# Layer norm 2 folded into centred expert and gate weights, in an attention and mixture-of-experts layer on one core

## Chip, cores and metric

The program runs on one core of a Trainium2 chip. Its time is the device time of one execution in microseconds (us). Engines are named as the profile names them: PE (TensorE matmul) and PEld (its weight load), DVE (VectorE), ACT (ScalarE), POOL (GpSimd), SP (SyncE, which issues most DMAs).

## What is computed

Four sequences of 1024 rows of 128 numbers (float32) pass one pre-norm layer:

```
x = x + attention(layernorm(x))      # 8 heads of 16; silu on q, k, v, u; silu(scores) for softmax; gated by silu(U)
x = x + ffn(layernorm(x))
# ffn: logits = xt @ w_gate.T ; top 2 of 8 ; softmax over the two -> gates
#      y = sum_e gates[:, e] * ((xt @ w_in[e].T) @ w_out[e].T)
# layernorm(x) = (x - mean) / sqrt(var + 1e-5), no scale or offset
```

An expert has no nonlinearity, so its two matrices can be multiplied once into one 128x128 matrix, and the FFN of a row is linear in the row apart from the choice and the gates.

## The kernel before

The 4096 rows are cut into nine units of query rows: two of 512 for each of batches 0 to 2, then 512, 256 and 256 for batch 3 (UNITS, numbered 0 to 8). Attention of a unit goes in groups: a group is one stretch of up to 512 columns of scores for four heads. There are 73 groups (units 0 to 8 have 5, 13, 5, 13, 5, 13, 5, 6 and 8). For each group PE makes four score tiles (scores, L623), DVE adds the relative bias where keys are near (add_bias, L914), ACT applies silu (weigh, L782 and L784), and PE multiplies by V (times_v, L639) into o_acc. DVE then gates a finished unit (gate_outputs, L929).

All other work is cut into jobs, and a table written out by hand (BEFORE, BESIDE, AFTER) says beside which group each job is issued. Every engine walks the same table in order, each with its own part of a job, and waits only on semaphores. In a group PE issues the scores of the next group's first two heads, times_v of the group before, the jobs, and then the other two heads. ACT runs the jobs of group i while it is in group i+1, between its two pairs of heads. On DVE the jobs that drain a PSUM bank come in group i; jobs without a bank (stats, norm, best, gates, split) come in group i+1, after the bias of the first pair of group i+2. POOL runs its parts strictly in the order of the table. Two PSUM banks (jobp) serve the jobs in turn, so a job of PE waits until the job two before it is drained.

The jobs that matter here:

- WT e, M e: transposes the output matrix of expert e and multiplies the two matrices into mm_e[:, e] (PE, copied by ACT at L850 and L854).
- T1, Q, K, V, U, MASK, split, REL: layer norm 1 transposed, projections, key mask, splitting of q and k, and the bias difference for far blocks (REL, POOL L583).
- SEL u: transposes the gated attention back and adds it to xs (PE L709, DVE L995). xs then holds the sum that layer norm 2 works on.
- stats2 u: mean and variance (DVE L953, L956), then on POOL rstd = (var + eps)^-0.5 and shift = -mean * rstd (function scale, L507 to L513).
- norm2 u: ACT writes xn2 = rstd * xs + shift (L797). For the last unit DVE only subtracts the mean (L969) and rstd is applied later (L1071, L1089).
- T2 u: PE transposes xn2 (L677), ACT copies to xn2T (L808).
- LOG u: logits (PE, DVE copy L1001). best u: top two, in two parts, with gap = top1 - top2 (DVE, L1063 to L1080). tanh u: ACT, L844. gates u: DVE, L1086 to L1092, which first waits for tanh.
- FF b t part: one tile of 128 rows times four experts (PE L648). DVE scales it by the gates into ymix (L1026), POOL adds the eight experts and xs (add_experts, L565 and L567). The last two tiles are done by DVE instead (MIX, mix_last, L1040), with no ymix.

Of the kernel before, what the change touches and what calls it, by code (L numbers as in the profile page):

```python
# [144 lines left out]
BESIDE = [
    [("T1", 0, 1), ("U", 0, 0), ("stats1", 1, 0), ("WT", 0)],
    [("M", 0), ("stats1", 1, 1), ("WT", 1)],
    [("Q", 0, 1), ("K", 0, 1), ("norm1", 1, 0), ("M", 1), ("V", 0, 1), ("T1", 1, 0), ("norm1", 1, 1)],
    [("K", 1, 0), ("Q", 1, 0)],
    [("WT", 2), ("split", 1, 0), ("REL",), ("U", 0, 1)],  # L150
    [("T1", 1, 1), ("WT", 3)],
    [("M", 2), ("SEL", 0), ("stats2", 0)],
    [("Q", 1, 1), ("MASK", 0, 1)],
    [("U", 1, 0), ("norm2", 0)],
    [("K", 1, 1), ("T2", 0), ("split", 1, 1)],
    [("WT", 4), ("M", 3)],
    [("LOG", 0), ("best", 0, 0), ("V", 1, 0), ("M", 4)],
    [("WT", 5), ("tanh", 0)],
    [("M", 5), ("WT", 6)],
    [("MASK", 1, 0), ("best", 0, 1)],  # L160
    [("gates", 0)],
    [("WT", 7)],
    [("stats1", 2, 0), ("MASK", 1, 1), ("M", 6)],
    [("M", 7), ("V", 1, 1), ("FF", 0, 0, 0), ("norm1", 2, 0), ("FF", 0, 0, 1), ("SEL", 1)],
    [("FF", 0, 1, 0), ("T1", 2, 0)],
    [("FF", 0, 1, 1), ("stats2", 1), ("U", 1, 1)],
    [("K", 2, 0), ("Q", 2, 0)],
    [("FF", 0, 2, 0), ("split", 2, 0), ("norm2", 1), ("stats1", 2, 1), ("FF", 0, 2, 1), ("V", 2, 0)],
    [("FF", 0, 3, 0), ("SEL", 2), ("T2", 1), ("best", 1, 0), ("stats2", 2), ("FF", 0, 3, 1), ("best", 1, 1),
     ("LOG", 1), ("norm1", 2, 1)],  # L170
    [("gates", 1), ("T1", 2, 1), ("tanh", 1), ("U", 2, 0)],
    [("FF", 0, 4, 0), ("norm2", 2), ("Q", 2, 1)],
    [("FF", 0, 4, 1), ("T2", 2)],
    [("K", 2, 1), ("LOG", 2), ("best", 2, 0)],
    [("best", 2, 1), ("MASK", 2, 0), ("gates", 2), ("FF", 0, 5, 0), ("stats1", 3, 0), ("tanh", 2), ("split", 2, 1)],
# [15 lines left out]
    [("gates", 3), ("K", 3, 1), ("MASK", 3, 0)],  # L191
    [("best", 4, 0), ("LOG", 4), ("FF", 1, 4, 0)],
    [("FF", 1, 4, 1), ("best", 4, 1), ("FF", 1, 5, 0)],
    [("FF", 1, 5, 1), ("split", 3, 1), ("tanh", 4)],
    [("gates", 4), ("FF", 1, 6, 0)],
    [("FF", 1, 6, 1), ("FF", 1, 7, 0)],
    [("FF", 1, 7, 1)],
    [("FF", 2, 0, 0)],
    [("FF", 2, 0, 1), ("FF", 2, 1, 0)],
    [("FF", 2, 1, 1), ("V", 3, 1)],  # L200
    [("FF", 2, 2, 0), ("stats2", 5), ("SEL", 5)],
    [("norm2", 5), ("FF", 2, 2, 1), ("FF", 2, 3, 0), ("MASK", 3, 1)],
    [("FF", 2, 3, 1), ("T2", 5)],
    [("best", 5, 0), ("best", 5, 1), ("LOG", 5), ("gates", 5)],
    [("FF", 2, 4, 0), ("tanh", 5), ("FF", 2, 4, 1)],
    [("FF", 2, 5, 0), ("U", 3, 1)],
    [("FF", 2, 5, 1), ("stats2", 6), ("SEL", 6)],
    [("FF", 2, 6, 0), ("FF", 2, 6, 1)],
    [("norm2", 6), ("FF", 2, 7, 0)],
    [("FF", 2, 7, 1), ("T2", 6)],  # L210
    [("best", 6, 0), ("best", 6, 1), ("LOG", 6), ("tanh", 6), ("gates", 6)],
    [("FF", 3, 0, 0), ("FF", 3, 0, 1)],
    [("FF", 3, 1, 0)],
    [("FF", 3, 1, 1), ("SEL", 7)],
    [("FF", 3, 2, 0), ("stats2", 7), ("FF", 3, 2, 1)],
    [("norm2", 7), ("FF", 3, 3, 0)],
    [("FF", 3, 3, 1), ("T2", 7)],
    [("LOG", 7), ("tanh", 7), ("best", 7, 0), ("best", 7, 1), ("gates", 7)],
# [2 lines left out]
AFTER = [
    [],
    [],
    [],
    [],
    [("SEL", 8), ("stats2", 8), ("norm2", 8), ("FF", 3, 5, 0), ("T2", 8), ("LOG", 8), ("best", 8, 0),
     ("best", 8, 1), ("gates", 8), ("FF", 3, 5, 1), ("FF", 3, 6, 0), ("FF", 3, 7, 0), ("FF", 3, 6, 1),
     ("FF", 3, 7, 1), ("tanh", 8), ("MIX",)],
    [],
    [],  # L230
# [926 lines left out]
```

## Time and profile before

| | us |
|---|---|
| median of 3 runs | 286.77 (285.39 to 286.88) |
| the profiled execution | 285.98 |
| its span, first to last instruction | 284.2 |
| PE busy | 263.2 (93% of the span) |
| DVE busy | 230.0 (81%) |
| ACT busy | 225.0 (79%) |
| POOL busy | 146.6 (52%) |

The span and the time of the same execution differ by 1.8 us, which lie outside the instructions. A busy share is an average over stages with different limits, and a busy PE is not PE at its peak.

### The profile page before, as it was taken

The numbers are of one execution on the slowest core, as the hardware profiler recorded it, in microseconds if no ns is written. First come the engines' busy times: TensorE is split into PE (matmuls) and PEld (weight loads), VectorE is DVE, ScalarE is ACT, GpSimd is POOL, SyncE is SP. The second block draws the span as 40 slices with busy tenths as digits, with TensorE's granted clock in tenths as the row PEclk, the third lists the DMA queues.
The fourth block names the chain that finished last, engine by engine and source line by source line (L and its number), as shares of the span: only waits on it lengthen the run. The fifth ranks groups of instructions, "written<-read, shape, count | busy, mean of one in ns | idle before, by whom it ended". The sixth has DMA issues, their size and how long they took to land.

```text
span 284.2 us, 8464 instructions
## 1 busy us (share of the span) xinstructions
PE 263.2 (93%) x3146; PEld 124.3 (44%) x3146; DVE 230.0 (81%) x764; ACT 225.0 (79%) x434; POOL 146.6 (52%) x236
## 2 busy tenths in 40 slices
...
GB/s 115 172 305 194 75 17 193 208 180 211 235 131 22 2 2 133 236 190 21 147 229 164 3 78 231 175 6 79 221 232 26 35 4 3 37 2 2 38 3 37
DMA packets 27912, 31.24 MB, mean 110 GB/s; under 512 B 3032, under 2 KB 16856, under 8 KB 27872
## 3 DMA queue, kind: packets, MB, share of 16 engines
...
q8 instruction: 25, 0.41, 0.6%
...
## 4 chain that ended last, share of the span: by engine, by line
PE 69%; DVE 16%; ACT 4%; DMA 4%; issue 3%; SPq 1%; POOL 1%; DVEq 0%; ACTq 0%; POOLq 0%
PE jobp L648 23%; PE o_acc L639 20%; PE score L623 20%; DVE score L914 9%; DMA wout_s<-in_L_ffn_w_out 3%; PE jobp L677 2%; DVE ymix L1026 2%; ACT wts L784 2%; PE jobp L709 2%; ACT xn L797 1%; PE jobp L729 1%; DVE xs L1040 1%; DVE stats L953 1%; SPq L452 1%; PE o_acc L743 1%
## 5 line engine op out<-in xcount | busy, mean ns | idle before, releaser
L914 DVE TENSOR_TENSOR score<-score,bias_near 128x256 f32<-128x256 f32 (+3 forms) x288 | 113.2, 468 | 13.7 <-PE score L623 13.3
L782 ACT ACTIVATE wts<-score 128x512 f32<-128x512 f32 (+1 forms) x172 | 96.7, 592 | 20.5 <-DVE score L914 16.5
L565 POOL TENSOR_TENSOR ymix<-ymix 128x512 f32<-128x512 f32 (+2 forms) x90 | 74.6, 829 | 48.6 <-DVE ymix L1026 43.9
L784 ACT ACTIVATE wts<-score,far 128x512 f32<-128x512 f32 x120 | 73.8, 700 | 6.6 <-DVE score L914 5.3
L639 PE MATMUL o_acc<-wts,v_pad 128*32 128x512 f32 (+3 forms) x864 | 77.1, 458 | 0.7 <-ACT wts L782 0.7
L648 PE MATMUL jobp<-mm_e,xn2T 128*32 128x512 f32 x480 | 60.3, 593 | 0.3 <-ACT mm_e L854 0.3
L623 PE MATMUL score<-q_stack,k_stack 64*128 64x256 f32 (+3 forms) x336 | 47.9, 356 | 0.1
L1026 DVE TENSOR_TENSOR ymix<-jobp,gates 128x512 f32<-128x512 f32 x60 | 40.3, 685 | 6.4 <-PE jobp L648 5.9
L623 PEld LDWEIGHTS score<-q_stack,k_stack 64*128 64x128 f32 x336 | 30.4, 184 | 31.0 <-issue 28.5
L639 PEld LDWEIGHTS o_acc<-wts,v_pad 128*32 128x32 f32 x864 | 20.8, 108 | 29.8 <-issue 16.1
L623 PE MATMUL score<-xn2T,xs 32*128 32x512 f32 (+3 forms) x192 | 26.9, 520 | 0.7 <-ACT wts L782 0.7
L797 ACT ACTIVATE xn<-xs,shift,rstd 128x128 f32<-128x128 f32 x58 | 24.0, 495 | 4.3 <-POOL shift L513 4.1
L507 POOL TENSOR_TENSOR rstd<-mv,eps_t 128x4 f32<-128x4 f32 (+1 forms) x17 | 3.5, 207 | 44.5 <-DVE mv L956 44.5
L648 PEld LDWEIGHTS jobp<-mm_e,xn2T 128*32 128x32 f32 x480 | 14.9, 110 | 20.9 <-issue 16.5
L914 DVE TENSOR_TENSOR score<-score,bias_rel 128x128 f32<-128x128 f32 (+1 forms) x48 | 14.4, 358 | 9.8 <-PE score L623 7.2
L553 POOL TENSOR_TENSOR v_pad<-v_s,kmask 128x256 f32<-128x256 f32 x16 | 9.8, 632 | 19.1 <-DVE kmask L989 16.2
L623 PEld LDWEIGHTS score<-xn2T,xs 32*128 32x128 f32 x192 | 14.3, 183 | 8.8 <-issue 5.7
L541 POOL TENSOR_TENSOR k_lo<-k,k_hi 128x512 fp32r<-128x512 f32 x6 | 8.1, 1342 | 16.7 <-DVE k_hi L1020 16.7
L512 POOL TENSOR_TENSOR rstd<-rstd,mhalf 128x4 f32<-128x4 f32 (+1 forms) x15 | 15.4, 1027 | 0.0
L567 POOL TENSOR_TENSOR xs<-xs,ymix 128x128 f32<-128x128 f32 x30 | 13.9, 463 | 2.3
L953 DVE BATCH_NORM_STATS2 stats<-xs 128x6 f32<-128x128 f32 x64 | 14.0, 279 | 0.4 <-DMA xs<-in_L_attn_x 0.2
L677 PE MATMUL jobp<-ident,xn 128*128 128x128 f32 x64 | 11.1, 295 | 3.1 <-DVE xn L969 1.1
...
## 6 DMA issues: line engine op xcount, KB each, us to landing
...
```

What stands on the lines that cost most here:

```text
L512: then_wait(pool.tensor_tensor(rstd[:, ln, ts], rstd[:, ln, ts], mhalf[:, ts], ALU.pow))
L565: then_wait(pool.tensor_tensor(y[:, 0:n], y[:, 0:n], y[:, n:2 * n], ALU.add))
L623: ins = pe.matmul(score[bank][:, c:c + n], keys, queries, start=True, stop=True)
L639: ins = pe.matmul(o_acc[32 * j:32 * j + 32, q0:q0 + n], v_pad[:, b % 2, kb, 4 * quad + j, :], wts[:, group % WTS, j, c:c + n], start=USES[ ...
L648: ins = pe.matmul(out[rows], lhsT[:, rows], rhs, start=start, stop=stop)
L677: ins = pe.transpose(bank[:, k * P:(k + 1) * P], src[:, t, :], ident[:])
L782: act.activation(weights, score[bank][:, 0:n], ACT.Silu, scale=HD ** -0.5).then_inc(weighed[bank], 1)
L784: act.activation(weights, score[bank][:, 0:n], ACT.Silu, bias=far[:, h:h + 1], scale=HD ** -0.5)\
L797: ins = act.activation((xn1, xn2)[ln][:, t], xs[:, b, t], ACT.Identity, bias=shift[:, ln, t:t + 1], scale=rstd[:, ln, t:t + 1])
L914: ins = dve.tensor_tensor(score[bank][:, c + near:c + n], score[bank][:, c + near:c + n], bias, ALU.add)
L953: ins = dve.bn_stats(stats[:, ln, t, :], xs[:, b, t, :])
L1026: drained_by(dve.tensor_tensor(y[:, es], bank_of(job)[:].rearrange("p (e d) -> p e d", d=D), gates[:, t, es].unsqueeze(2).to_broadcast([P, ...
```

## The change

Layer norm 2 is no longer computed on the rows. With centre = I - 1/128, centring commutes with the linear maps: (x - mean) @ M = x @ (centre @ M). So the merged expert matrices and the gate weights are multiplied by centre once (three new jobs, CM 0 and CM 1 for four experts each, CM 2 for the gate weights). T2 then transposes xs itself and needs only SEL. The factor rstd of a row is positive and so leaves the choice of experts as it is. It is put on gap (ahead of tanh) and on the picked gates, as was done before for the last unit alone. The norm2 jobs, the tile xn2 and the shift of layer norm 2 are gone. The table of jobs is written anew.

```diff
-                if (args, ln) in [((LAST,), 1), ((0, 0), 0)]:
+                if ln or args == (0, 0):
                     pool.tensor_tensor(rstd[:, ln, ts], rstd[:, ln, ts], mhalf[:, ts], ALU.pow).then_inc(scaled, 1)
                     return
...
+            then_wait(pool.memset(centre[:], -1.0 / D))
+            pool.affine_select(out=centre[:], in_=centre[:], compare_op=ALU.not_equal, fill=1.0 - 1.0 / D, base=0,
+                               pattern=[[-1, P]], channel_multiplier=1).then_inc(centre_set, 1)
...
-                        pe.wait_ge(ready, count)
+                        wait_drained(pe, ("SEL",) + args)
                     for k, t in enumerate(tiles):
-                        ins = pe.transpose(bank[:, k * P:(k + 1) * P], src[:, t, :], ident[:])
+                        ins = pe.transpose(bank[:, k * P:(k + 1) * P], xn1[:, t] if kind == "T1" else xs[:, b, t], ident[:])
...
+                elif kind == "CM":
+                    k = args[0]
+                    pe.wait_ge(centre_set, 1)
+                    if k < 2:
+                        for e in range(k * E // 2, (k + 1) * E // 2):
+                            wait_drained(pe, ("M", e))
+                        ins = quarters(bank[:], centre[:], mm_e[:, k * E // 2:(k + 1) * E // 2].rearrange("p e d -> p (e d)"))
+                    else:
+                        pe.wait_ge(wg_in, 16)
+                        ins = quarters(bank[:, 0:E], centre[:], wg_s[:])
...
+                elif kind == "CM":
+                    k = args[0]
+                    wait_filled(act, job)
+                    if k < 2:
+                        drained_by(act.copy(mm_e[:, k * E // 2:(k + 1) * E // 2].rearrange("p e d -> p (e d)"), bank_of(job)[:]), job)
+                    else:
+                        drained_by(act.copy(wg_c[:], bank_of(job)[:, 0:E]), job)
...
                     ins = dve.tensor_tensor(gap[:, ts], top[:, 0, ts, 0], top[:, 0, ts, 1], ALU.subtract)
-                    if u == LAST:
-                        dve.wait_ge(scaled, SCALES.index(((LAST,), 1)) + 1)
-                        then_wait(ins)
-                        ins = dve.tensor_tensor(gap[:, ts], gap[:, ts], rstd[:, 1, ts], ALU.mult)
-                    ins.then_inc(top_ready, 1)
+                    dve.wait_ge(scaled, SCALES.index(((u,), 1)) + 1)
+                    then_wait(ins)
+                    dve.tensor_tensor(gap[:, ts], gap[:, ts], rstd[:, 1, ts], ALU.mult).then_inc(top_ready, 1)
```

The first of the two CM branches is PE's, the second ACT's. The same is done in gates: the product with rstd (L1089) is now made for every unit. The table, in short:

```diff
 BEFORE (ahead of group 0)
-    stats1 0 0, RB, norm1 0 0, stats1 0 1, T1 0 0, Q 0 0, K 0 0, norm1 0 1, V 0 0, MASK 0 0
+    stats1 0 0, RB, T1 0 0, norm1 0 0, norm1 0 1, stats1 0 1, Q 0 0, K 0 0, T1 0 1, V 0 0, K 0 1, Q 0 1, MASK 0 0, REL
 BESIDE, groups 0 to 2
-    T1 0 1, U 0 0, stats1 1 0, WT 0 | M 0, stats1 1 1, WT 1 | Q 0 1, K 0 1, norm1 1 0, M 1, V 0 1, T1 1 0, norm1 1 1
+    stats1 1 0, WT 0 | M 0, WT 1, stats1 1 1 | CM 2, U 0 0, norm1 1 0, M 1, U 0 1, T1 1 0, norm1 1 1
 BESIDE, groups 22 to 27
-    ... norm2 1 ... | FF 0 3 0, SEL 2, T2 1, best 1 0, stats2 2, FF 0 3 1, best 1 1, LOG 1, norm1 2 1 |
-    gates 1, T1 2 1, tanh 1, U 2 0 | FF 0 4 0, norm2 2, Q 2 1 | FF 0 4 1, T2 2 | K 2 1, LOG 2, best 2 0
+    FF 0 2 0, FF 0 2 1 | FF 0 3 0, norm1 2 1, stats2 2, SEL 2 | FF 0 3 1, LOG 1, best 1 0, best 1 1, gates 1 |
+    V 2 0, U 1 1, T2 2, T1 2 1, FF 0 4 0, tanh 1, FF 0 4 1 | FF 0 5 0, FF 0 5 1, MASK 2 0 | FF 0 6 0, K 2 1
 BESIDE, last groups
-    FF 3 3 1, T2 7 | LOG 7, tanh 7, best 7 0, best 7 1, gates 7 | FF 3 4 0, FF 3 4 1
+    FF 3 1 1, FF 3 2 0, LOG 7, best 7 0 | FF 3 2 1, FF 3 3 0 | FF 3 3 1, best 7 1 | gates 7, tanh 7 | FF 3 4 0, FF 3 4 1
 AFTER
-    SEL 8, stats2 8, norm2 8, FF 3 5 0, T2 8, LOG 8, best 8 0, best 8 1, gates 8, FF 3 5 1, ... , tanh 8, MIX
+    FF 3 5 0, SEL 8, T2 8, stats2 8, LOG 8, best 8 0, best 8 1, gates 8, FF 3 5 1, ... , MIX, tanh 8
```

Counted over units 0 to 8, the number of FF jobs beside the groups is 0, 0, 6, 12, 4, 14, 6, 6, 10 before and 0, 2, 4, 14, 4, 12, 5, 7, 10 after. CM 0 and CM 1 stand in unit 1, CM 2 in unit 0.

## Rows read from the trace of the kernel before

**Rows 1.** The page, part 1: busy time, share of the span, instructions.

```profile
PE 263.2 (93%) x3146; PEld 124.3 (44%) x3146; DVE 230.0 (81%) x764; ACT 225.0 (79%) x434; POOL 146.6 (52%) x236
```

**Rows 2.** The page, part 4: the chain that ended last, by engine.

```profile
PE 69%; DVE 16%; ACT 4%; DMA 4%; issue 3%; SPq 1%; POOL 1%; DVEq 0%; ACTq 0%; POOLq 0%
```

**Rows 3.** Windows: stretches of units 0, 3, 6, 8: length, PE, PEld, DVE, ACT, POOL busy.

```profile
22.10:43.10 21.00, 19.18 (x265) 9.86 (x262) 13.20 (x44) 19.02 (x39) 6.31 (x11) 1.00 0.33 89
...
107.70:151.90 44.20, 43.64 (x470) 17.45 (x462) 40.65 (x137) 42.08 (x84) 30.74 (x48) 1.00 0.69 166
...
210.40:230.30 19.90, 17.20 (x212) 8.00 (x212) 19.15 (x66) 13.49 (x27) 10.42 (x17) 1.00 0.23 59
...
248.60:270.40 21.80, 20.56 (x268) 10.46 (x264) 19.29 (x63) 16.39 (x32) 12.93 (x20) 1.00 0.05 15
```

**Rows 4.** Groups of instructions by line and shape: count, busy us, mean ns, idle before.

```profile
L797 ACT ACTIVATE xn<-xs,shift,rstd 128x128 f32<-128x128 f32 x58 | 24.0, 495 | 4.3 <-POOL shift L513 4.1
...
L808 ACT COPY xn2T<-jobp 128x512 f32<-128x512 f32 x7 | 4.2, 602 | 0.1
```

**Rows 5.** Chain that ended last, in order of time: start us, us, what.

```profile
112.85 0.89 DVE lg L1066 x4
...
117.57 1.27 ACT wts L784 x2
118.84 1.29 ACT xn L797 x4
...
140.52 1.72 PE jobp L648 x16
...
218.16 0.87 ACT xn L797 x2
...
266.19 1.07 DVE score L914 x4
...
270.46 0.34 DVE oT L929
```

**Rows 6.** Timeline of the start: start us, us, instruction, idle before it.

```profile
13.72 3.82 DVE L914 TENSOR_TENSOR score<-score,bias_near 128x512 f32<-128x512 f32 x8 [0.85 <-PE score L623]
...
20.48 0.63 PE L729 MATMUL jobp<-ident,wout_s 128*128 128x128 f32 x4 [1.24 <-DMA wout_s<-in_L_ffn_w_out]
...
21.14 0.91 SPq L461 DMA_DIRECT2D wg_s<-in_L_ffn_w_gate  x1
...
22.20 2.02 DVE L914 TENSOR_TENSOR score<-score,bias_near 128x384 f32<-128x384 f32 x5 [4.67 <-PE score L623]
...
26.86 1.04 PE L648 MATMUL jobp<-xn1T,wq_s 128*32 128x512 f32 x8
```

**Rows 7.** DMA issues: KB each, median us from issue to landing.

```profile
wg_s<-in_L_ffn_w_gate SPq DMA_DIRECT2D x1, 4.0 KB, 5.4
```

**Rows 8.** Timeline of the end: start us, us, instruction, idle before it.

```profile
269.00 0.86 PE L639 MATMUL o_acc<-wts,v_pad 128*32 128x256 f32 x16 [0.38 <-ACT wts L782]
...
270.61 2.64 POOL L565 TENSOR_TENSOR ymix<-ymix 128x512 f32<-128x512 f32 x3 [3.42 <-DVE ymix L1026]
...
271.38 0.42 DVE L995 TENSOR_TENSOR xs<-xs,jobp 128x256 f32<-128x256 f32 x1 [0.59 <-PE jobp L709]
...
273.47 0.41 PE L677 MATMUL jobp<-ident,xn 128*128 128x128 f32 x2 [1.13 <-DVE xn L969]
...
274.01 0.71 POOL L509 TENSOR_TENSOR rstd<-rstd,mhalf 128x2 f32<-128x2 f32 x1
...
275.57 0.15 DVE L1067 TENSOR_TENSOR gap<-top 128x2 f32<-128x2 f32 x1
275.83 0.16 DVE L1071 TENSOR_TENSOR gap<-gap,rstd 128x2 f32<-128x2 f32 x1
...
277.39 0.69 DVE L1026 TENSOR_TENSOR ymix<-jobp,gates 128x512 f32<-128x512 f32 x1
...
278.00 4.22 DVE L1040 SCALAR_TENSOR_TENSOR xs<-score,gates,xs 128x128 f32<-128x128 f32 x16
```

More of the change, by code:

```diff
@@ L148 @@
-    [("Q", 0, 1), ("K", 0, 1), ("norm1", 1, 0), ("M", 1), ("V", 0, 1), ("T1", 1, 0), ("norm1", 1, 1)],
+    [("stats1", 1, 0), ("WT", 0)],
+    [("M", 0), ("WT", 1), ("stats1", 1, 1)],
+    [("CM", 2), ("U", 0, 0), ("norm1", 1, 0), ("M", 1), ("U", 0, 1), ("T1", 1, 0), ("norm1", 1, 1)],
     [("K", 1, 0), ("Q", 1, 0)],
[L150 to L175, printed above, removed]
[15 rows of a table removed]
@@ L191 @@
[L191 to L218, printed above, removed]
+    [("split", 1, 0), ("V", 0, 1), ("T1", 1, 1)],
+    [("Q", 1, 1)],
+    [("SEL", 0), ("WT", 2)],
+    [("MASK", 0, 1), ("stats2", 0), ("T2", 0), ("WT", 3)],
+    [("K", 1, 1)],
+    [("M", 2), ("M", 3)],
+    [("LOG", 0), ("CM", 0), ("split", 1, 1), ("V", 1, 0), ("best", 0, 0)],
[13 rows of a table added]
+    [("FF", 0, 3, 1), ("LOG", 1), ("best", 1, 0), ("best", 1, 1), ("gates", 1)],
@@ new lines @@
+    [("V", 2, 0), ("U", 1, 1), ("T2", 2), ("T1", 2, 1), ("FF", 0, 4, 0), ("tanh", 1), ("FF", 0, 4, 1)],
+    [("FF", 0, 5, 0), ("FF", 0, 5, 1), ("MASK", 2, 0)],
+    [("FF", 0, 6, 0), ("K", 2, 1)],
+    [("best", 2, 0), ("LOG", 2), ("stats1", 3, 0), ("V", 2, 1), ("Q", 2, 1), ("best", 2, 1), ("stats1", 3, 1)],
+    [("tanh", 2), ("FF", 0, 6, 1), ("MASK", 2, 1), ("split", 2, 1)],
+    [("U", 2, 0), ("norm1", 3, 0), ("gates", 2), ("FF", 0, 7, 0)],
+    [("FF", 0, 7, 1), ("FF", 1, 0, 0)],
+    [("FF", 1, 0, 1)],
@@ new lines @@
+    [("U", 2, 1)],
+    [("FF", 1, 1, 0), ("norm1", 3, 1), ("FF", 1, 1, 1)],
+    [("T1", 3, 0), ("T1", 3, 1)],
+    [("K", 3, 0)],
+    [("FF", 1, 2, 0), ("SEL", 3)],
+    [("FF", 1, 2, 1), ("T2", 3)],
+    [("stats2", 3), ("FF", 1, 3, 0), ("U", 3, 0)],
+    [("LOG", 3), ("FF", 1, 3, 1)],
+    [("best", 3, 0), ("Q", 3, 0), ("SEL", 4)],
+    [("tanh", 3), ("best", 3, 1), ("gates", 3), ("split", 3, 0), ("T2", 4)],
+    [("stats2", 4), ("V", 3, 0)],
+    [("K", 3, 1), ("LOG", 4)],
+    [("FF", 1, 4, 0), ("FF", 1, 4, 1)],
@@ new lines @@
+    [("FF", 1, 5, 0), ("best", 4, 0), ("Q", 3, 1), ("best", 4, 1), ("split", 3, 1)],
+    [("FF", 1, 5, 1), ("tanh", 4), ("FF", 1, 6, 0)],
+    [("gates", 4), ("FF", 1, 6, 1), ("MASK", 3, 0)],
+    [("FF", 1, 7, 0), ("FF", 1, 7, 1)],
+    [("FF", 2, 0, 0), ("MASK", 3, 1)],
+    [("FF", 2, 0, 1)],
+    [("FF", 2, 1, 0), ("V", 3, 1)],
+    [("FF", 2, 1, 1)],
+    [("FF", 2, 2, 0), ("FF", 2, 2, 1)],
+    [("SEL", 5), ("FF", 2, 3, 0), ("stats2", 5)],
+    [("T2", 5)],
+    [("best", 5, 0), ("tanh", 5), ("LOG", 5), ("U", 3, 1), ("best", 5, 1), ("gates", 5)],
[4 rows of a table added]
@@ L219 @@
+    [],
+    [("FF", 2, 7, 0), ("best", 6, 0), ("best", 6, 1), ("gates", 6)],
+    [("FF", 2, 7, 1), ("tanh", 6)],
+    [("FF", 3, 0, 0)],
+    [("FF", 3, 0, 1), ("stats2", 7), ("SEL", 7)],
+    [("FF", 3, 1, 0), ("T2", 7)],
+    [("FF", 3, 1, 1), ("FF", 3, 2, 0), ("LOG", 7), ("best", 7, 0)],
+    [("FF", 3, 2, 1), ("FF", 3, 3, 0)],
+    [("FF", 3, 3, 1), ("best", 7, 1)],
+    [("gates", 7), ("tanh", 7)],
     [("FF", 3, 4, 0), ("FF", 3, 4, 1)],
@@ L223 @@
     [],
[L224 to L228, printed above, removed]
+    [("FF", 3, 5, 0), ("SEL", 8), ("T2", 8), ("stats2", 8), ("LOG", 8), ("best", 8, 0), ("best", 8, 1),
+     ("gates", 8), ("FF", 3, 5, 1), ("FF", 3, 6, 0), ("FF", 3, 7, 0)],
     [],
@@ L233 @@
     [],
+    [("FF", 3, 6, 1), ("FF", 3, 7, 1)],
+    [("MIX",), ("tanh", 8)],
 ]
@@ L289, in build @@
         wq_s, wk_s, wv_s, wu_s = sb("wq_s", [P, D]), sb("wk_s", [P, D]), sb("wv_s", [P, D]), sb("wu_s", [P, D])
[L290 removed]
+        wg_s, wg_c = sb("wg_s", [P, E]), sb("wg_c", [P, E])
+        centre = sb("centre", [P, P])
         ident = sb("ident", [P, P])
```

66 lines of the change are left out of this document (26 added, 40 removed), and 31 rows, old and new, of the table BESIDE.

## Prediction, made before the changed kernel was run

> **What bounds the kernel now.** I read the page first. PE is busy for 263.2 of 284.2 us, DVE and ACT for about 80% each [rows 1], so no engine is far from full, and the share of a mean doesn't say which one sets the time. The chain that ended last does it better: 69% of it is PE, 16% DVE, 4% ACT and 1% POOL [rows 2]. The reader is to see that time taken from ACT alone is mostly time off the path, and that time put on PE is mostly on it.
>
> Then the windows, cut at the gating of each unit [rows 3]. Unit 0 (22.1 to 43.1 us) has 1.8 us of idle PE. Unit 3 (107.7 to 151.9) has all three engines at 92 to 99%: PE 43.64, ACT 42.08, DVE 40.65 of 44.2. In unit 6 PE falls to 17.2 of 19.9 and DVE leads with 19.15. In unit 8 both are near full again. Behind 270.4 us comes a tail in which one small step follows another. So I look for the change in four places: the start, the places where norm2 lies on the chain, the last two groups, and the tail.
>
> **What is taken off.** Norm2 has 4 tiles for each of 7 units and 2 for unit 7 on ACT: 30 of the 58 instructions of line 797. They hold ACT for 24.0/58 = 0.414 us each (their mean of 495 ns overlaps) [rows 4], which makes 12.4 us. CM puts back two copies of 128x512 at 0.60 us [rows 4] and a tiny one, 1.4 us at most. ACT is 11 us lighter. Little of it counts directly. I find norm2 on the chain twice: 1.29 us at 118.84 (unit 2, with two silus of 1.27 us just ahead of it in ACT's queue), and from 218.16 with 0.87 us (unit 5) [rows 5]. The first I take in full, 1.3 us. At the second PE is held by DVE as well, so I take 0.4 us. Together **-1.7 us**; between 0 (the silu behind it is then held by DVE) and the 11 us of ACT.
>
> POOL loses two of four small instructions per unit; it is 52% busy and gains no time for the path.
>
> **What is put on.** CM 0 and CM 1 have the shape of an FF job. Two of those take 1.72 us on a busy PE [rows 5], so 0.86 each; CM 2 has 8 columns and at most 0.1. That is 1.8 us on PE. With PE on 69% of the chain I count 69% of it: **+1.3 us** (0 to 1.8). DVE gets, in units 0 to 7, a product with rstd on gap (0.16 us), the wait ahead of it (gap ends at 275.72, the product starts at 275.83: 0.11) and a second product of the kind, on pick (0.16) [rows 8]: 0.43 us for each of 8 units, 3.4 us. The wide ones (four tiles) have no row; the two-tile row is the nearest. DVE is on 16% of the chain: **+0.6 us** (0 to 3.4, the upper end if DVE bounds throughout).
>
> The Trainium skill ("VectorE: DVE Perf Modes", section on the TRN2 errata) gives an SBUF-to-SBUF operation 58 cycles and one per element at 0.96 GHz. By that a product of 2 or 4 columns would be an estimated 0.065 us and the sixteen some 1.1 us with no waits. The rows of this case show 0.16 us for 2 columns, and the sum goes by them.
>
> best now also waits for POOL's rstd. In every unit but the last, stats2 stands at least one whole group ahead of best in the table, and POOL waits there for nothing but DVE, so I price it at nothing. If that cover goes, POOL may have one add_experts ahead of it, about 3.1 us (2.64 for its first three adds from 270.61; rstd's power starts at 274.01) [rows 8]; queued behind best on DVE are the bias of the next heads and the FF scalings, for which ACT and PE wait.
>
> **The start.** WT 0 waits for its weights until 20.48 us, in both kernels, since SP's queue is unchanged. DVE idles 4.67 us ahead of 22.20, behind scores that PE issues after WT 0 [rows 6]. The new table puts K 0 1, Q 0 1 and T1 0 1 ahead of group 0, so the first bias starts some 3.6 us later than 13.72; the eight bias instructions of 3.82 us then end near 21.1, still ahead of 22.20. What has been moved there is hidden. Group 2 then holds neither Q nor K nor V, but U twice and CM 2. ACT's jobs ahead of T1 1 0 were Q, K, abs of K and V at 0.60 each, four norms at 0.41 and M at 0.27, 4.3 us; they are now U twice, the norms, M and CM 2, 3.3. PE had waited for these. I take **-1.0 us** (0 to -2, with the 1.8 us of idle PE as the limit [rows 3]). CM 2 needs wg_s, which is issued at 21.14 and lands 5.4 us later [rows 6, 7], at 26.5 to 27.5; PE came to group 2's jobs at 26.86. That may cost up to 0.6 us, and all behind it in PE's queue would wait. The centre matrix delays POOL's fill of bias_near by some 0.5 us, which the later first bias covers. REL, moved up, is through before its first reader.
>
> **The table in the middle.** PE's job work beside the groups, with 0.86 us for FF, Q, K, U, V, M and 0.6 for transposes, stays within 0.5 us in sum, but unit 2 loses 2.8 us and unit 3 gains 3.7 (two more FF jobs, one V, one U). Unit 3 was full. Its ACT part falls only by 0.5 us. If it gets longer by 3.7 while unit 2, where DVE is nearly full too, gives back the 1.4 by which its DVE jobs shrink, the net is +2.3; if both balance it is 0. I take it as 0, and keep +2.3.
>
> **The last two groups.** DVE's last bias ends at 267.26; then come best 7 and gates 7, two FF scalings, and only at 270.46 the gating of unit 8 [rows 5], which PE had made possible at 269.86 [rows 8]. The new table has best 7 0 three groups earlier and best 7 1 one, which takes DVE's longest part out of this stretch. The 0.5 us comes back at the gating, and I add 0.4 for the norm2, T2 and LOG of unit 7 that leave these groups: **-0.9 us** (0 to -2).
>
> **The tail.** Before: add at 271.38, then stats, centring, and T2 only at 273.47. After: T2 can follow at 271.9, which is 1.55 us earlier, and stats runs beside the transpose and its copy [rows 8]. But rstd now is late: POOL is in add_experts of the FF before it from 270.61 and has rstd at 274.72. The product on gap, at 275.83 before, could come at 274.3 and must wait until 274.8. So 1.0 us remains: **-1.0 us** (-0.5 to -1.55). MIX (4.22 us) and the FF scaling ahead of it (0.69) stay [rows 8].
>
> Sum: -1.7 + 1.3 + 0.6 - 1.0 + 0 - 0.9 - 1.0 = **-2.7 us**. The profiled execution took 285.98 us, 1.8 of it outside its span of 284.2; after, 283.3 with a span of 281.5. It lay 0.8 us under the median of the three runs, so against the median the forecast is 286.77 - 2.7 = **284.1 us**.
>
> **Rivals.**
>
> *Larger gain.* ACT was 95% busy in unit 3 and 91% in unit 0 [rows 3]. ACT's 4% of the chain are 11.4 us [rows 2]. If DVE and PE stalls there come from ACT's queue rather than from their own work, half of these, 5.7 us, may go in place of my 1.7. That is 4 us more: 280.1 us. For it: the silus at 117.57 wait behind bias work and norm. Against: the other half of ACT's chain is silu that stays, and all 5.7 us would have to be queueing.
>
> *No difference.* The folding does what it says and yet PE, with 1.8 us more, sets the pace: norm2's two places are filled by the next-late thing (DVE's 0.89 us of best at 112.85 lies just ahead of the first [rows 5]), unit 3 takes its 2.3 us. Sum -2.7 + 1.7 + 0.9 = 286.7 or so.
>
> *Slower: DVE waits for tanh.* gates 1 now stands one group ahead of tanh 1, and gates 6 ahead of tanh 6. DVE, in gates, then waits until ACT has done the other pair and the next group's first pair of silus (four at 0.63, from the 1.27 for two [rows 5]) and, for unit 1, V, U, T2 and T1 at 0.6 each: 4.9 us, against the 3.3 us of best that DVE does meanwhile. That is 1.6 us for unit 1 and about nothing for unit 6. With DVE's 3.4 us wholly on the path (+2.8 on my sum) and this 1.6, the time is 288.5 us. It decides once more than 4.1 us come on top of the -2.7. Queued behind gates are the bias of the next pair and the drains of PE's banks. For it: 16% of the chain is DVE and unit 6 shows it at 96% of its time [rows 3]. Against: in most stretches PE leads.
>
> By the Trainium skill ("Perfetto Trace Analysis", Identifying the Most-Contended Engine) PE's matmul share is no measure, and DVE, at 81% the fullest of the others, would be the engine to relieve; this change loads it. By that the outcome is this rival's. The chain's 69% on PE speaks against.
>
> **How the numbers follow.** My forecast, between 281.5 and 285.3: 0.50. Larger gain: 0.14. No difference: 0.20. Slower: 0.16. A measurement of this kernel tells about 0.5%, 1.4 us, from no change. Faster by more than that (under 285.3): 0.64; within: 0.20; slower (over 288.2): 0.16. The range leaves out most of the slower rival and the lower half of the larger gain: **280.0 to 288.0 us**.
>
> **What would show it.** Right: line 797 at 28 instructions and ACT near 214 us busy; two 0.86 us CM jobs in unit 1; T2 8 within 0.2 us of the add of unit 8, and the product on gap waiting for POOL; the silu of group 0 later and group 2 shorter; the last gating not held by FF scalings. Wrong: DVE idle with gates or the gap product named as what stood there; PE idle over 1 us at CM 2; unit 3 longer than 45.5 us; the chain's DVE share over 20%.

## The result, and the profile after

| | before | changed |
|---|---|---|
| median | 287.06 us (285.11 to 290.86, 20 runs) | 284.57 us (283.46 to 287.55, 20 runs) |
| ratio | | 0.9938 [0.9917, 0.9958] |
| span of the profiled execution | 284.2 | 281.6 |

The changed kernel is 0.62% faster, 1.8 us by the ratio (1.2 to 2.4 by its interval). I had forecast 2.7 us (284.1 us). The median is near the forecast; the gain is about two thirds of it, and the terms of the sum are mostly not the measured ones. That the sum came out near is luck, as the experiments show.

The page of the changed kernel, part 1, and its chain by engine, which answer to [rows 1, 2]:

```profile
PE 263.0 (93%) x3170; PEld 125.0 (44%) x3170; DVE 233.2 (83%) x778; ACT 216.0 (77%) x407; POOL 143.8 (51%) x222
...
PE 59%; DVE 25%; ACT 8%; issue 4%; POOL 2%; DMA 1%; SPq 0%; DVEq 0%; ACTq 0%; POOLq 0%
```

ACT lost 9 us and DVE gained 3.2. PE has 24 more matmuls and is no busier. The chain moved from PE (69% before) to DVE (16% before) and ACT (4%). A DVE share over 20% was one of my four signs of a wrong prediction, and all four came: DVE's share is 25%, unit 3 took 46.50 us (over 45.5), PE stood 1.54 us at CM 2, and DVE stood 0.55 us ahead of gates 1.

The same stretches as in [rows 3], cut at the changed kernel's gatings (units 0, 3, 6, 8; columns as there):

```profile
22.10:42.25 20.15, 18.37 (x265) 9.67 (x268) 12.02 (x43) 18.35 (x39) 5.75 (x11) 1.00 0.37 93
105.95:152.45 46.50, 45.90 (x536) 18.86 (x528) 42.87 (x145) 40.56 (x79) 33.86 (x50) 1.00 0.58 140
208.86:227.69 18.83, 17.16 (x184) 8.05 (x184) 18.45 (x67) 12.45 (x24) 8.05 (x12) 1.00 0.12 32
247.08:268.80 21.72, 21.18 (x276) 10.53 (x276) 20.18 (x65) 15.35 (x29) 15.60 (x22) 1.00 0.09 26
```

Unit 3 is 2.3 us longer and unit 6 1.1 shorter. So I compare by stage: the length from one unit's gating on DVE to the next. A stage is the difference of two starts in the timeline. There are nine traces with the new table and five with the old one; each is given where it says something. In the two traces of the changed kernel the stages from unit 2 to unit 8 repeat to 0.02 us, and unit 1 took 47.58 and 48.00. In the table, norm2 out means the kernel before without norm2 and without CM.

| stage, us | before | changed | e11: norm2 out | e12: and no products | e1: fold, old table |
|---|---|---|---|---|---|
| start, to gating 0 | 43.10 | 42.25 | 44.04 | 43.72 | 42.33 |
| unit 1 | 46.10 | 47.58 | 45.98 | 46.01 | 48.14 |
| unit 2 | 18.54 | 16.12 | 18.55 | 18.54 | 20.44 |
| unit 3 | 44.16 | 46.50 | 44.27 | 43.57 | 44.26 |
| unit 4 | 15.51 | 15.01 | 15.50 | 15.51 | 15.50 |
| unit 5 | 43.00 | 41.40 | 42.71 | 42.36 | 42.71 |
| unit 6 | 19.92 | 18.83 | 20.02 | 21.32 | 20.02 |
| unit 7 | 18.29 | 19.39 | 18.18 | 18.01 | 18.18 |
| unit 8 | 21.76 | 21.72 | 22.04 | 21.85 | 22.01 |
| tail | 13.8 | 12.8 | 12.8 | 12.8 | 12.8 |

Between the two profiled executions the 2.6 us are 0.85 at the start, 0.73 in units 1 to 8, and 1.0 in the tail. The 0.85 is nearly all clock (next section); what the change itself took off is 1.4 to 1.8 us.

### The profile page after: what moved, and what is told of

It reads as the page before. It is cut to its first block, busy times and chain, and to the rows that moved or that the text cites. A ratio compares the mean times of both kernels' runs of the same rounds, so it can differ in the third digit from the quotient of the medians.

```text
span 281.6 us, 8492 instructions
## 1 busy us (share of the span) xinstructions
PE 263.0 (93%) x3170; PEld 125.0 (44%) x3170; DVE 233.2 (83%) x778; ACT 216.0 (77%) x407; POOL 143.8 (51%) x222
## 4 chain that ended last, share of the span: by engine, by line
PE 59%; DVE 25%; ACT 8%; issue 4%; POOL 2%; DMA 1%; SPq 0%; DVEq 0%; ACTq 0%; POOLq 0%
PE jobp L652 22%; PE o_acc L643 16%; PE score L627 16%; DVE score L933 16%; DVE ymix L1037 4%; ACT wts L798 2%; PE jobp L680 2%; ACT xn L810 2%; ACT wts L796 1%; DVE xs L1051 1%; DVE stats L972 1%; PE jobp L732 1%; PE jobp L712 1%; DMA xs<-in_L_attn_x 1%; POOL rstd L512 1%
## 5 line engine op out<-in xcount | busy, mean ns | idle before, releaser
L796 ACT ACTIVATE wts<-score 128x512 f32<-128x512 f32 (+1 forms) x172 | 98.0, 589 | 30.7 <-DVE score L933 25.8
L627 PE MATMUL score<-q_stack,k_stack 64*128 64x256 f32 (+3 forms) x336 | 50.4, 355 | 0.9 <-ACT wts L796 0.4
L627 PEld LDWEIGHTS score<-q_stack,k_stack 64*128 64x128 f32 x336 | 31.0, 184 | 33.3 <-issue 28.3
L627 PE MATMUL score<-xn2T,xs 32*128 32x512 f32 (+3 forms) x192 | 25.6, 519 | 0.7 <-ACT wts L796 0.7
L627 PEld LDWEIGHTS score<-xn2T,xs 32*128 32x128 f32 x192 | 13.5, 183 | 7.7 <-issue 5.1
L571 POOL TENSOR_TENSOR xs<-xs,ymix 128x128 f32<-128x128 f32 x30 | 13.8, 459 | 2.4
L810 ACT ACTIVATE xn<-xs,shift,rstd 128x128 f32<-128x128 f32 x28 | 11.5, 487 | 1.7 <-POOL shift L513 1.7
L509 POOL TENSOR_TENSOR rstd<-rstd,mhalf 128x4 f32<-128x4 f32 (+1 forms) x10 | 9.5, 953 | 0.8
L652 PE MATMUL jobp<-xn1T,wq_s 128*32 128x512 f32 x64 | 8.4, 593 | 0.8 <-ACT xn1T L820 0.8
```

Of the source, the lines that this page charges most:

```text
L571: pool.tensor_tensor(xs[:, b, t], xs[:, b, t], y[:, 0], ALU.add).then_inc(tile_done, 1)
L627: ins = pe.matmul(score[bank][:, c:c + n], keys, queries, start=True, stop=True)
L652: ins = pe.matmul(out[rows], lhsT[:, rows], rhs, start=start, stop=stop)
L796: act.activation(weights, score[bank][:, 0:n], ACT.Silu, scale=HD ** -0.5).then_inc(weighed[bank], 1)
L810: ins = act.activation(xn1[:, t], xs[:, b, t], ACT.Identity, bias=shift[:, t:t + 1], scale=rstd[:, 0, t:t + 1])
```

## The experiments

**The same kernel again**, for the spread between runs.

> The changed kernel once more, unaltered, as the reference for the three kernels beside it. Its stages should repeat within 0.3 us each against its first profile: unit 3 46.5 us long (44.2 before), unit 2 16.1 (18.5 before), tail from the last gating to the end 12.8 (13.8 before). Ratio to before 0.990 to 0.996.

285.83 us against 287.23 of the kernel before, ratio 0.9963 [0.993, 0.9996], span 284.4. This second measurement puts the gain at 1.1 us, just outside the range that I expected. Units 2 to 8 are those of the table to 0.02 us; the first gating came at 44.60 instead of 42.25, and unit 1 took 0.42 us more, over the 0.3 that I allowed. The difference between these two traces is thus in the start and unit 1. PE's granted clock was 0.50 and 0.70 in 20 to 28 us here, and 1.00 in the first trace of the same kernel. The same kind of dip separates the first traces of the two kernels (windows: length, then PE, PEld, DVE, ACT, POOL, granted clock, DMA share, GB/s); first the changed kernel, then the kernel before:

```profile
16.00:20.00 4.00, 3.35 (x37) 1.90 (x33) 3.51 (x9) 2.88 (x6) 2.85 (x3) 1.00 1.04 310
20.00:24.00 4.00, 4.00 (x53) 2.35 (x56) 3.63 (x11) 3.74 (x8) 2.11 (x2) 1.00 0.97 279
```

```profile
16.00:20.00 4.00, 3.24 (x15) 0.95 (x13) 1.54 (x5) 3.11 (x6) 0.00 (x0) 0.57 0.97 307
20.00:24.00 4.00, 3.52 (x57) 2.23 (x57) 1.80 (x5) 1.52 (x3) 0.00 (x0) 1.00 1.01 291
```

The kernel before had PE at 1.2 GHz for nearly all of 16 to 20 us. The trace of the old table that had no such dip (e1) gates unit 0 at 42.33, and the changed kernel at 42.25. The jobs ahead of that gating are in e1 those of the kernel before. So of the 0.85 us at the start 0.77 is the clock, and 0.08 is left for the jobs there.

**The fold without the new table.** Norm2 leaves the old table, CM 2 stands beside group 5, CM 0 beside group 11, CM 1 beside group 18.

```diff
-    ("V", 1, 0), ("M", 4)]
+    ("V", 1, 0), ("CM", 0), ("M", 4)]
...
-    [("M", 7), ("V", 1, 1), ("FF", 0, 0, 0)
+    [("M", 7), ("V", 1, 1), ("CM", 1), ("FF", 0, 0, 0)
```

> The folding alone: the table of before, with the norm2 jobs taken out, CM 2 put beside group 5, CM 0 beside group 11 and CM 1 beside group 18. Theory A (the folding brings the gain by what it takes off the path, in two norm2 places and the tail, and the table only the start and the last groups): 1.3 to 2 us under before, ratio 0.993 to 0.996, tail 1.5 to 1.6 us shorter than before since SEL 8 stays ahead of FF 3 5 0, units 3 and 6 shorter by 1.3 and 0.4. Rival B (the folding saves nothing by itself, because PE and DVE get more work, and the new table does it): ratio 0.998 to 1.004.

292.29 us, ratio 1.0168 [1.0111, 1.0225]: slower, which neither theory expected. Units 3 to 8 sum to the same as before to 0.04 us, the tail has its 1.0, and units 1 and 2 lose 3.9. The traced run was the fastest of the six (288.63 us at a mean clock of 0.996); the others took 290.17 to 292.73 at 0.976 to 0.988, so the ratio holds some clock that no trace shows, beside the stages' 3.9. The chain of this kernel at CM 1:

```profile
89.90 0.27 ACT mm_e L875
90.17 0.14 issue
90.30 1.10 PE jobp L654 x8
91.40 0.02 issue
91.43 0.60 ACT mm_e L869
92.02 0.14 issue
92.16 1.02 PE jobp L654 x5
```

PE, ACT, PE: M 7 is drained, CM 1 waits for it (0.38 us idle), is copied, and the first FF waits for the copy (0.79 idle), while everything behind in PE's queue waits too. Against e11 below, which has no CM in the same table, unit 1 is 2.2 us longer and unit 2 1.9. In the changed kernel CM 1 runs at 80.10, is copied at 82.64, and its first reader starts at 83.54 with no stand.

**CM shrunk.** CM 0 and CM 1 multiply and copy 8 columns into a tile that nobody reads, so the expert matrices stay uncentred.

```diff
-    ins = quarters(bank[:], centre[:], mm_e[:, ...])
+    ins = quarters(bank[:, 0:E], centre[:], mm_e[:, k * E // 2, 0:E])
...
-    drained_by(act.copy(mm_e[:, ...], bank_of(job)[:]), job)
+    drained_by(act.copy(cm_out[:], bank_of(job)[:, 0:E]), job)
```

> The changed kernel with CM 0 and CM 1 cut to 8 columns each, so that the jobs, their waits and their places stay and 1.7 us of PE work and 1.2 us of ACT copies go; the expert matrices stay uncentred, so the output lacks that part. Theory A (PE leads in unit 1, as priced at 69%): unit 1 (47.6 us long) gets 1.2 to 1.8 us shorter, the rest stays within 0.3. Rival (the copies and products fit beside ACT's and DVE's work): at most 0.5 us.

285.57 us, ratio 0.996 [0.9931, 0.9988]. Unit 1 took 47.70 (47.58 and 48.00 with the full CM); units 2 to 8 are the same to 0.02. The edit takes some 1.6 us of work off PE, an estimate: two jobs of 0.86 us, less 0.06 us each, the time from CM 2's start to the next job's in the changed kernel (26.87 and 26.93). These 1.6 us were thus worth nothing to 0.3 us, which is less than unit 1 repeats by. The jobs, their waits and their banks stay in this kernel; what those cost in the new table no run shows.

**Norm2 taken out of the old table, nothing put in its place but the products.** No CM, so the matrices are uncentred.

```diff
-    [("U", 1, 0), ("norm2", 0)],
+    [("U", 1, 0)],
```

(and so for the other eight; fold, products and tail as in the changed kernel)

> The kernel before with norm2 taken out and the rstd products put in, T2 reading xs, and nothing else: table, banks and queues as before, no CM (logits and experts use uncentred weights, so the output lacks the centring). Theory (the folding in its own place is worth nothing between the gatings, since the other engines fill it, and only the tail gains): each unit from 1 to 8 within 0.3 us of before, tail 1.0 shorter; then the 4 us that the kernel with CM in the old table lost in units 1 and 2 are all CM's waits. My prediction's term (norm2 on the chain, 1.3 us in unit 3 and 0.4 in unit 6): these two shorter by that.

285.78 us, ratio 0.9957 [0.9928, 0.9987]. Units 1 to 8 sum to 227.25 us, before 227.28: norm2 out and products in cancel. The tail gives 1.0, and so does the measurement (1.2 by the ratio). This theory held in every stage, and my 1.3 us for unit 3 did not show.

**And the products out too**: gap and pick of units 0 to 7 are not multiplied by rstd, so their gates lack it.

```diff
-    dve.wait_ge(scaled, SCALES.index(((u,), 1)) + 1)
-    then_wait(ins)
-    dve.tensor_tensor(gap[:, ts], gap[:, ts], rstd[:, 1, ts], ALU.mult).then_inc(top_ready, 1)
+    if u == LAST:
+        ...
+    ins.then_inc(top_ready, 1)
```

> Table and banks of the kernel before, norm2 taken out of it, no CM jobs (so the matrices are not centred), and no product with rstd on gap and pick in units 0 to 7 (their gates lack rstd). So it is the kernel before with the 28 norm2 activations of units 0 to 7 gone and the tail's changes, and nothing put on. With the products, the same table took 45.98, 18.55, 44.27, 15.50, 42.71, 20.02, 18.18 and 22.04 us in units 1 to 8, 227.25 in sum, against 227.28 of the kernel before. Theory A (norm2 was worth about 1.3 us in unit 3 and 0.4 in unit 6, and the products took it back): unit 3 at 43.0 or less, unit 6 at 19.5, sum of units 1 to 8 1.0 to 1.7 us under 227.25. Theory B (in the old table norm2's time on ACT was covered by PE and DVE and worth nothing, and the products too): every unit within 0.3 us of the one with the products, sum 226.9 to 227.5. In both the tail is 12.8 us.

284.67 us, ratio 0.9911 [0.9869, 0.9953]. ACT has 30 activations less than before, and not the 28 of the expectation. In size Theory A holds, unit 6 set aside; in place it does not, since unit 3 was to be at 43.0 or less and took 43.57. Against the kernel before, norm2 alone is worth 0.59 us in unit 3, 0.64 in 5, 0.28 in 7, and nothing in 1, 2, 4 and 8 (-0.09, 0, 0, +0.09): 1.5 us. Against e11, the products cost 0.70 in unit 3, 0.35 in 5, 0.17 in 7, 0.19 in 8: 1.4 us. Unit 6 is left out of both sums, since it is 1.3 us longer here for another reason, with these windows:

```profile
213.70:217.70 4.00, 2.36 (x40) 0.84 (x32) 3.88 (x15) 1.35 (x4) 1.94 (x3) 0.94 0.01 2
217.70:221.70 4.00, 4.00 (x34) 1.74 (x28) 2.58 (x6) 2.69 (x5) 3.42 (x7) 0.63 0.01 4
```

against the kernel before in the same place:

```profile
214.40:218.40 4.00, 2.36 (x42) 0.94 (x34) 3.87 (x15) 1.60 (x4) 1.85 (x5) 1.00 0.03 7
218.40:222.40 4.00, 3.78 (x40) 1.89 (x36) 3.84 (x11) 4.00 (x10) 3.77 (x7) 1.00 0.00 0
```

PE had the same 2.36 us of work in the four us ahead; once the clock fell behind it and once it did not. It fell in unit 6 in two of five traces of the old table (here and in e10, where the unit took 21.28 us), and in none of nine of the new one.

**Products out of the new table.** The same edit in the changed kernel.

> The changed kernel without the products with rstd on gap and pick in units 0 to 7, and without DVE's wait for rstd there; the gates of those units lack the factor. Theory A (DVE on 16% of the chain, as priced): 0.6 us faster than the changed kernel. Rival C (DVE has become the bound; its share of the chain in the changed kernel is 25%): 1.5 to 3.4 us faster, most of it in units 3, 5 and 6.

285.81 us, ratio 0.9962 [0.9928, 0.9995]. Unit 5 was 0.27 us shorter, 6 0.37 and 7 0.61, unit 8 0.36 longer, and unit 1 between 0.36 and 0.78 shorter. That makes 1.3 to 1.7 us in the stages, though unit 1 does not repeat better than 0.4 us. The median doesn't show it. In this trace the tail took 13.93 us, 1.1 more than in the changed kernel, with a clock of 0.58 in 274 to 278 us where the changed kernel was granted 1.00; the first gating came at 45.44; and the interval can't tell 1 us. Whether the other runs have the dip in the tail as well is not shown.

**ACT's relief put back.** In the changed kernel ACT gets 30 activations that nobody reads, ahead of the copies of T2.

```diff
+    if kind == "T2" and args != (LAST,):
+        for k in range(len(tiles)):
+            act.activation(idle_out[:, k], centre[:], ACT.Identity, scale=1.0)
```

> The changed kernel with 30 idle ACT instructions of 128x128 (28 before the T2 copies of units 0 to 6 and 2 of unit 7), that is ACT's load of norm2 put back without its place in the chain of waits. Theory A (ACT's lighter load itself counts for little, at most 1 us): ratio to before 0.990 to 0.997. Rival (ACT's queue was what held unit 3): 2.5 to 5 us slower than the changed kernel, ratio 1.000 to 1.010, units 1 and 3 longer by 1 us or more each.

288.84 us, ratio 1.0059 [1.0019, 1.0098]. The 6.8 us of such work (4.5 more on the page, part 1) lengthen unit 3 by 0.8, 2 by 0.8, 5 by 0.5, 7 by 0.4 and unit 1 by 0.1 to 0.5: 2.6 to 3.0 us in all, and 2.8 by the two ratios. That is the rival's price, without its place (1 us or more in unit 1). In the old table all of norm2 was worth 1.5 us, so ACT was nearly covered there; the new table leans on its relief, as the chain's 8% of ACT says too. Taken at the copies of T2 alone, it says nothing of other places.

**Tanh ahead of gates.** Tanh 1 and tanh 6 go into the group of their gates.

```diff
-    ("best", 1, 1), ("gates", 1)],
+    ("best", 1, 1), ("tanh", 1), ("gates", 1)],
```

> The changed kernel with tanh 1 and tanh 6 moved to the group of their gates, one group earlier; only ACT's order changes. The slower rival of the prediction put 1.6 us on tanh 1 and nothing on tanh 6; in the trace of the changed kernel DVE stood 0.55 us ahead of gates 1. Theory: DVE's stand vanishes and unit 3 (46.5 us) gets 0 to 0.5 us shorter. If DVE's wait there were what makes unit 3 longer than the 44.2 us of before: 1 us or more.

292.37 us, ratio 1.0188 [1.0138, 1.0238]: 4.4 us more in unit 3, 0.7 in 7, 0.9 in 8, where I had expected unit 3 to get shorter. ACT now stands for DVE's gap with silus behind it. First the timeline of ACT in this kernel, then of DVE in the changed one:

```profile
112.70 2.41 ACT L798 ACTIVATE wts<-score,far 128x512 f32<-128x512 f32 x4
118.22 0.20 ACT L856 ACTIVATE half_tanh<-gap 128x4 f32<-128x4 f32 x1 [3.12 <-DVE gap L1082]
118.33 2.41 ACT L798 ACTIVATE wts<-score,far 128x512 f32<-128x512 f32 x4
```

```profile
115.30 0.19 DVE L1090 TENSOR_TENSOR pick<-lg,top 128x32 f32<-128x32 f32 x1
116.05 0.19 DVE L1096 SCALAR_TENSOR_TENSOR pick<-pick,half_tanh 128x32 f32<-128x32 f32 x1 [0.55 <-ACT half_tanh L856]
```

PE ran dry behind it, and the clock fell (windows of this kernel):

```profile
116.00:120.00 4.00, 1.80 (x44) 0.89 (x35) 3.69 (x20) 1.78 (x4) 2.47 (x4) 1.00 0.99 246
120.00:124.00 4.00, 2.72 (x12) 1.77 (x16) 0.04 (x1) 2.89 (x6) 0.00 (x0) 0.63 1.07 221
```

So the stand of my rival exists (DVE waits for tanh 1), but is 0.55 us and not 1.6. The other order costs 4.4 us there, a part of which is the clock; the two are not separated. Whether the 0.55 us is a part of what makes unit 3 longer than before, this run can't tell.

**CM 2 three groups later**, beside group 5 and not 2.

```diff
-    [("CM", 2), ("U", 0, 0), ("norm1", 1, 0)
+    [("U", 0, 0), ("norm1", 1, 0)
...
-    [("Q", 1, 1)],
+    [("Q", 1, 1), ("CM", 2)],
```

> The changed kernel with CM 2 moved from group 2 to group 5, away from the start, where PE stands 1.54 us until ACT has drained it. Theory A (CM 2 holds a bank in the busiest place of the start): the time of the first gating, 42.25 us at full clock, comes 0.3 to 1 us earlier. Rival (M 1 then waits for the drain of another job of the same queue): no change within 0.2 us. The first gating is to be read beside the granted clock.

285.71 us, ratio 0.9946 [0.9917, 0.9975]; unit 1 47.22. In the changed kernel PE issues CM 2 at 26.87, its copy comes only at 29.30 in ACT's queue, and PE, whose next use of that bank is M 1, stands 1.54 us. In e7 M 1 starts at 30.26 with no stand, and PE stands 1.16 us for the bank after it, at 32.48 behind ACT's copy of U. I had expected the first gating 0.3 to 1 us earlier; it came at 44.72, behind a clock of 0.50 in 20 to 24 us, so this run can't tell. Unit 1 is 0.4 to 0.8 us shorter (0.4 to 0.8 in e9 too, which builds on this), and why is not shown: e3, with CM 2 in its old place, has 47.22 as well. The ratios of e7 and e9 lie between the two measurements of the changed kernel (0.9938 and 0.9963): not shown to be faster.

**Spare matmuls at the start**, to hold the clock. In e8: two ahead of Q 0 0, five ahead of T1 0 1, two ahead of WT 0, and in AFTER SEL 8 first and FF 3 5 0 behind T2 8.

```diff
+    if job == ("Q", 0, 0):
+        keep_busy(2)
...
+    if job == ("T1", 0, 1):
+        keep_busy(5)
...
-    [("FF", 3, 5, 0), ("SEL", 8), ("T2", 8), ("stats2", 8), ("LOG", 8)
+    [("SEL", 8), ("stats2", 8), ("T2", 8), ("FF", 3, 5, 0), ("LOG", 8)
```

> The changed kernel with idle products of the identity (into o_acc, which is not in use yet) where PE otherwise stands: 2 ahead of Q 0 0, 5 ahead of T1 0 1, 2 ahead of WT 0. And in the tail T2 8 is issued ahead of FF 3 5 0. Theory (what moves the time from run to run is the granted clock between 16 and 28 us: 0.50 to 1.00 there in four traces, and the first gating between 42.3 and 45.4 us; it fell after PE's gaps at 8 to 20 us): the mean clock of all runs 0.99 or more, first gating near 42.3 us, median 1.5 to 2 us under the changed kernel's. Rival (the clock falls whatever PE does there): same spread and median. Tail: T2 8 0.5 us earlier, but LOG 8 stands behind FF 3 5 0 and rstd behind POOL's adds, so the end comes at most 0.3 us earlier.

285.91 us, ratio 0.997 [0.9945, 0.9994]. The mean granted clock was 0.990 to 0.999 in all twelve runs (e0: 0.984 to 0.996), and 1.00 up to 64 us in the trace, so it was held there, but the first gating came at 43.10, 0.85 late: the five spare matmuls ahead of T1 0 1 stand behind the wait for a bank (idle until 12.51 us). The median that I had expected, 1.5 to 2 us lower, did not come. The tail is 0.3 us longer, because DVE's scaling of FF 3 5 0 now stands ahead of its copy for LOG 8.

e9 is e7 with two and five of them, the five ahead of the wait for the bank:

> The changed kernel with CM 2 in group 5 and idle products of the identity (2 ahead of Q 0 0, 5 ahead of T1 0 1) issued ahead of the wait for the bank, so that they fill 1.8 us of PE's stand and hold up nothing. Theory: mean clock 0.99 or more, first gating 42.3 us, unit 1 0.4 us shorter than in the changed kernel, span 281 in most runs; ratio to before 0.983 to 0.990. Rival (filling the gaps ahead of 13 us does not keep the clock at 16 to 28 us): spread and ratio as without.

286.09 us, ratio 0.9944 [0.9908, 0.998]; the granted clock in 20 to 28 us was 0.64 and 0.51, so it was not held, and nothing was won over e7. The rival held.

e10 is the kernel before with six ahead of WT 0:

> The kernel before with 6 idle products of the identity ahead of WT 0, where PE stands 2 us until the weights land. Theory (the granted clock falls after such a stand and costs 1 to 2.5 us in most runs): mean clock 0.99 or more in most runs, first gating near 42.3 us instead of 43.1 and later, median 1 to 2 us under before. Rival (no link): same clocks and median.

288.36 us, ratio 1.0019 [0.9979, 1.0059]. The clock fell to 0.50 in 16 to 20 us all the same. My theory of what holds it fell in both, and what does stays open.

## Why the sum was near and its terms were not

| term | forecast | measured |
|---|---|---|
| norm2 off the chain | -1.7 | -1.5 (e12 against before, old table) |
| CM on PE | +1.3 | 0 to +0.3 (e4; the size of the jobs, not their waits) |
| products on DVE | +0.6 | +1.4 (e12 and e11); 1.3 to 1.7 (e3) |
| start | -1.0 | -0.1 at equal clock; -0.85 in the two profiles |
| table in the middle | 0 | -0.7 or -0.3 (changed or e0, less e11, units 1 to 8, CM and last groups within) |
| last groups | -0.9 | -0.3 in unit 8 against e11 (in the row above); 0.0 against before |
| tail | -1.0 | -1.0 |

The measured terms add up to 1.5 to 1.9 us off; by the stages, with the start at equal clock, it is 1.4 to 1.8, and not 2.7. That the spans differ by 2.6 is due to the dip at the start of the trace of before (0.8 us). No run has the new table with norm2 kept, so what the table is worth is known only with the fold in it.

**Norm2.** The size held: 1.5 us come from 8.5 us less of ACT on the page, in e12 without CM (I had counted 12.4; with CM I had counted 11, and the page shows 9.0). The place did not. I read two pieces of the chain of one execution as if they were the stages that would give; unit 3 gave 0.6 of the 1.3, and units 5 and 7 the rest.

**CM and products: the step that failed.** I priced both by the engine's share of the chain that ended last: 69% for PE, 16% for DVE. The 1.6 us of PE work taken out in e4 cost at most 0.3. DVE's products, 2.1 us of busy time between e12 and e11, cost 1.4. The rows held for their length (0.164 and 0.181 us in the median, on L1082 and L1098 of the changed kernel); the share did not. The one error is 1.0 to 1.3 us, the other 0.8, and they have opposite signs: that they cancel is luck. The chain names the last link at each step; PE work can be on that chain and still be nearly free, if another engine would be late without it; that DVE is this other engine here is argued from its 16% before and 25% after, and not shown. The Trainium skill ("Perfetto Trace Analysis", Identifying the Most-Contended Engine) says that matmul busy time is no measure of how full PE is, and to go by occupancy for the others. By marginal price the runs agree: of a us put on DVE in the old table some 65% arrived, of one on PE in the new table at most a fifth, and of one taken from ACT in the old table 18%. ACT's price is not fixed, though: of the 4.5 us more on the page of e2, put on in the new table, some 60% arrived. The outcome that I tied to that rule did not come, because the products cost 1.4 us and not the 3.4 of that rival, less than norm2 and the tail gave together.

**The start.** The 3.3 us of ACT jobs that replace 4.3 gave 0.1 us at equal clock, and CM 2's late bank made PE stand 1.54 us at 29.51, which I had bounded at 0.6 by the transfer of its weights and should have bounded by its copy's place in ACT's queue. What I had called hidden (the first bias at 17.55, done at 21.4, ahead of the next) was.

**The middle.** The balance was the right call. Unit 3 did pass 45.5 us, but unit 2 gave back 2.4 us and not the 1.4 that I allowed; over units 1 to 8 the new table takes 0.3 to 0.7 less than the old one while it carries CM. What the new table does above all is to place CM: units 1 to 8 of e1, with CM at the one set of places tried in the old table, take 4.3 to 4.7 us more.

**The last groups.** The gating of unit 8 is indeed no longer held: o_acc is ready at 268.71 and gated at 268.80. Unit 8 is 0.04 us shorter than before and 0.3 shorter than in e11, which like it has the products. Unit 7 is 1.1 longer and unit 6 1.1 shorter, one FF job having moved from 6 to 7. The three together took 59.94 us against 59.97 before. I took the stand for a gain; with the products added, most of it did not show.

**The tail.** 1.0 us, but by another account. The timeline of the changed kernel, which answers to [rows 8]:

```profile
268.80 0.41 DVE L948 TENSOR_TENSOR oT<-o_acc,uT 128x256 f32<-128x256 f32 x1
...
269.70 0.69 DVE L1037 TENSOR_TENSOR ymix<-jobp,gates 128x512 f32<-128x512 f32 x1 [0.48 <-PE jobp L652]
270.31 0.41 DVE L1006 TENSOR_TENSOR xs<-xs,jobp 128x256 f32<-128x256 f32 x1
...
270.87 0.41 PE L680 MATMUL jobp<-ident,xs 128*128 128x128 f32 x2 [0.92 <-DVE xs L1006]
...
272.40 0.71 POOL L509 TENSOR_TENSOR rstd<-rstd,mhalf 128x2 f32<-128x2 f32 x1
...
272.97 0.15 DVE L1078 TENSOR_TENSOR gap<-top 128x2 f32<-128x2 f32 x1
273.23 0.16 DVE L1082 TENSOR_TENSOR gap<-gap,rstd 128x2 f32<-128x2 f32 x1
```

From the add to T2 it is 0.56 us against 2.09 before: -1.53, and I had 1.55. From the gating to the add it is 1.51 against 1.00: +0.5, since FF 3 5 0 now stands ahead of SEL 8 on PE and its scaling ahead of the add on DVE, a move that I left unpriced. Behind T2 both take 10.73. The wait for rstd that I put in place of this did not show: POOL is done at 273.11, just ahead of the gap at 273.12. Where SEL 8 stays first (e1) T2 starts 0.17 earlier and the wait is there, as small as this (the kernel of e1):

```profile
277.94 0.16 DVE L1084 TENSOR_TENSOR gap<-gap,rstd 128x2 f32<-128x2 f32 x1 [0.16 <-POOL rstd L511]
```

So the two orders give the same tail, 12.8 us. My size was right, by an account of which one part was missing and another did not come.

**Time outside the span** was 1.74 us on average in 29 runs of the kernel before and 2.08 in the 20 of the changed one; I had taken it as equal. It is 1.78 in e11 and e12, which have no CM, and 2.10 in e7, but 1.82 in e8, which has it: left open. It takes 0.3 us off the 2.6 of the spans.

**The clock** is in the result as well. Over all runs its mean was 0.986 for the kernel before (99 runs, mean span 285.4) and 0.993 for the changed one (32 runs, 283.2). Among the 99, a clock lower by 0.01 goes with 1.8 us more. By that, of the 2.2 us between the mean spans up to 1.2 would be fewer dips; by the stages at equal clock it would be 0.4 to 0.8. The shortest span of each kernel, 282.9 us and 281.2, differ by 1.7, which is what the stages say. The new table has more PE work in unit 6, where the old one dips in two of five traces. At the start it has more too (3.34 us against 3.08 in 12 to 16 us), but the clock fell there in six of its nine traces, in e9 with 3.63 us of work in that stretch. No run held the clock by itself at no cost, so this share is argued, and not shown.

**The rivals.** "Larger gain" fell: ACT was worth 1.5 us, not 5.7. "No difference" was nearer than its chance says: the body changed by 0.3 to 0.7 us only, and nearly all of what is certain is the tail. Its sum was not the one that its words give: they name unit 3's 2.3 us, and the sum gives back 0.9; with the 2.3 it would have been 288.1 us. "Slower" named an engine that did take 1.4 us; its wait for tanh was 0.55 us, a third of its price.
